# Attention's value weight multiplied by its output weight once on chip: the read comes out by tokens, the output product and its copy are left out, and all queues stand in a new order

## The reference, cut to what matters

```python
x = x + 0.5 * _L0_ffn_ref(_layernorm(x), ...)      # int8 product
x = x + _L0_attn_ref(_layernorm(x), ...)           # recurrence, then its feed-forward
x = x + 0.5 * _L0_ffn_ref(_layernorm(x), ...)
x = x + 0.5 * _L1_ffn_ref(_layernorm(x), ...)      # experts, pass 0
x = x + _L1_attn_ref(_layernorm(x), ...)
x = x + 0.5 * _L1_ffn_ref(_layernorm(x), ...)      # experts, pass 1
```

```python
q = hidden_state @ Wq + bq
k = jax.nn.sigmoid(hidden_state @ Wk + bk)
g = jax.nn.sigmoid(hidden_state @ Wg + bg)
v = hidden_state @ Wv + bv
def step(state, xs):
    qi, ki, vi, gi = xs
    state = state * gi[:, :, None] + ki[:, :, None] * vi[:, None, :]
    return (state, jnp.einsum('bk,bkv->bv', qi, state))
state, outs = jax.lax.scan(step, init, xs)
out = jnp.swapaxes(outs, 0, 1) @ Wo + bo
```

## Time and profile before

| | |
|---|---|
| median of 3 runs | 701.86 us (701.73 to 702.95) |
| profiled execution, first to last instruction | 703.3 us |
| instructions | 14597 |
| PE busy, PEld busy | 616.8 us (88%), 487.0 us (69%) |
| DVE, ACT, POOL busy | 487.2, 398.0, 387.9 us |
| mean granted clock of PE | 0.974 |
| chain that ended last, by engine | PE 59%, DVE 10%, ACT 9%, issue 7%, DMA 6% |

### The profile page before, as it was taken

One profiled execution on the slowest core, in us unless ns is written; L12 is line 12 of the kernel. 1 busy time (PEld: TensorE's weight loads), 2 busy tenths in 40 slices (PEclk: granted clock), 3 DMA queues, 4 the chain that ended last, 5 costly groups with the idle time before them and its releaser, 6 DMA issues.

```text
span 703.3 us, 14597 instructions
## 1 busy us (share of the span) xinstructions
PE 616.8 (88%) x4232; PEld 487.0 (69%) x4232; DVE 487.2 (69%) x1730; ACT 398.0 (57%) x1036; POOL 387.9 (55%) x416
## 2 busy tenths in 40 slices
PE   1478999999799989899986998899999999987971
PEld 1234565566566888788885886779878998776970
DVE  6986777878889867554625996878865874546334
ACT  3477887999686454554445556464665446343530
POOL 4425434435747787767653413651865764766642
PEclk9699999999999999999999999999999999999996
DMA  7998000000042366577668010214324545566886
GB/s 263 410 411 342 1 0 1 1 1 20 31 107 61 95 179 179 168 214 223 189 200 286 22 66 11 63 46 117 89 73 134 157 115 161 166 197 175 251 302 214
DMA packets 60126, 100.99 MB, mean 144 GB/s; under 512 B 10288, under 2 KB 28592, under 8 KB 59792
## 3 DMA queue, kind: packets, MB, share of 16 engines
q1 hardware_dynamic: 50832, 81.52, 37.7%
q0 software_dynamic: 8640, 17.84, 7.1%
q10 hardware_dynamic: 576, 0.69, 0.3%
HBM read 61.79 MB, written 38.23 MB: 142 GB/s over the span
## 4 chain that ended last, share of the span: by engine, by line
PE 59%; DVE 10%; ACT 9%; issue 7%; DMA 6%; POOL 5%; SPq 4%; POOLq 0%; ACTq 0%; DVEq 0%
PE bank L1071 14%; PE bank L1048 7%; PE bank L1282 4%; PE bank L934 3%; DMA tin<-rows_by_expert 3%; PE bank L959 3%; PE bank L308 3%; PE bank L945 3%; PE bank L510 3%; PE bank L663 3%; PE bank L313 3%; POOL rows_by_expert L830 2%; PE bank L677 2%; PE bank L1054 2%; PE bank L692 2%
## 5 line engine op out<-in xcount | busy, mean ns | idle before, releaser
L830 POOL DMA_INDIRECT rows_by_expert<-xx,sidx x128 | 126.3, 987 | 71.7 <-DVE xx L809 35.8
L1071 PE MATMUL bank<-tint,twt 128*128 128x128 f32 x1136 | 150.7, 278 | 10.9 <-DVE thidt L1109 5.7
L1071 PEld LDWEIGHTS bank<-tint,twt 128*128 128x128 f32 x1136 | 138.6, 192 | 26.3 <-issue 13.6
L1109 DVE TENSOR_TENSOR thidt<-tsil,bank 128x256 f32<-128x256 f32 x142 | 58.9, 419 | 98.6 <-ACT tsil L1087 86.6
L1120 POOL DMA_INDIRECT rows_done<-tout,tin x98 | 95.4, 974 | 52.4 <-ACT tout L1095 28.3
L1087 ACT ACTIVATE tsil<-bank 128x256 f32<-128x256 f32 x142 | 54.4, 384 | 82.1 <-PE bank L1071 80.4
L1048 PE MATMUL bank<-e_dn,thidt 128*128 x568 | 89.8, 283 | 7.3 <-issue 3.5
L1048 PEld LDWEIGHTS bank<-e_dn,thidt 128*128 128x128 f32 x568 | 76.4, 193 | 19.4 <-issue 18.8
L1095 ACT ACTIVATE tout<-bank,tin 128x128 f32<-128x128 f32 x142 | 51.5, 367 | 35.1 <-PE bank L1054 33.7
L1120 POOL DMA_INDIRECT rows_done<-tout,tdst x44 | 43.8, 996 | 30.1 <-issue 11.8
L1080 ACT ACTIVATE tint<-bank 128x128 f32<-128x128 f32 x142 | 38.2, 275 | 37.1 <-PE bank L1054 36.8
(11 more groups left out here) (271 smaller groups left out, 1363.9 us busy)
## 6 DMA issues: line engine op xcount, KB each, us to landing
twt<-moe_gu SPq DMA_DIRECT2D x142, 256.0 KB
rows_by_expert<-tout SPq DMA_DIRECT2D x25, 715.0 KB, 19.6
tin<-rows_by_expert SPq DMA_DIRECT2D x142, 65.0 KB
hid<-rows_done SPq DMA_DIRECT2D x12, 512.0 KB, 4.8
x<-x_in SPq DMA_DIRECT2D x8, 256.0 KB, 4.1
rows_by_expert<-xx,sidx POOLq DMA_INDIRECT x128
out<-x SPq DMA_DIRECT2D x8, 256.0 KB, 3.5
rows_done<-tout,tin POOLq DMA_INDIRECT x98, 3.0
```

The lines of the kernel that those rows point to most:

```text
L830: pool.indirect_dma_start(out=rows_by_expert, out_offset=bass.IndirectOffsetOnAxis(ap=sidx[h][:, k:k + 1], axis=0), in_=xx[h][:, r, t, :], ...
L1071: m = pe.matmul(bank[UP_BANKS[p][j]][:, c * P:(c + 1) * P], weights[:, c * P:(c + 1) * P], tint[g % TURNS][:, :], start=True, stop=True)
L1109: dve.tensor_tensor(thidt[g % TURNS][:, :, :].rearrange("p j c -> p (j c)"), tsil[g % TURNS][:, :], bank[UP_BANKS[p][j]][:, INNER:2 * INNE ...
```

## The change

`w_vo` holds the product of the value weight and the output weight (128 x 128) and, in each of its 128 rows, the value bias times the output weight. It is made once, on chip: two transposes (`k_vturn_tensor`), a copy, two products (`k_fold_tensor`) and a copy, between helpers of units 6 and 7 of the feed-forward block. `g_value_tensor` and `g_value_vector` use it in place of the value weight and bias. `g_read_tensor` exchanges its operands, so that the result comes out by tokens; `g_read_scalar` and `g_out_tensor` are gone, and `g_add_vector` adds the read's bank. `g_turn_tensor` now waits for that addition.

```diff
+        w_vo = sb("w_vo", [P, 2, P])
...
+            elif p == 0:
+                pe.wait_ge(s_voc, 2)
...
             if u >= 2:
-                pe.wait_ge(s_oc, n(u) - 2)
+                pe.wait_ge(s_x, n(u) - 2)
             transposes(pe, gb(u, 0), tt[u % 2], ident).then_inc(s_gtr, 1)
...
-                m = pe.matmul(gb(u, 0)[:, t * P:(t + 1) * P], gxt[u % 2][:, t * P:(t + 1) * P], a_sq[:, 2, :],
+                m = pe.matmul(gb(u, 0)[:, t * P:(t + 1) * P], gxt[u % 2][:, t * P:(t + 1) * P], w_vo[:, 0, :],
...
-                pe.matmul(gb(u, 0)[:, c0:c0 + P], v[:, c0:c0 + P], at[h][:, c0:c0 + P], start=True, stop=True)
-                pe.matmul(gb(u, 0)[:, c1:c1 + P], v[:, c0:c0 + P], across[h][:, b, :], start=True, stop=False)
-                m = pe.matmul(gb(u, 0)[:, c1:c1 + P], v[:, c1:c1 + P], at[h][:, c1:c1 + P], start=False, stop=True)
+                pe.matmul(gb(u, 0)[:, c0:c0 + P], at[h][:, c0:c0 + P], v[:, c0:c0 + P], start=True, stop=True)
+                pe.matmul(gb(u, 0)[:, c1:c1 + P], across[h][:, b, :], v[:, c0:c0 + P], start=True, stop=False)
+                m = pe.matmul(gb(u, 0)[:, c1:c1 + P], at[h][:, c1:c1 + P], v[:, c1:c1 + P], start=False, stop=True)
...
-        def g_read_scalar(act, u):
-            act.wait_ge(s_o, n(u))
-            if u >= 2:
-                act.wait_ge(s_op, n(u) - 2)
-            act.activation(bufE[u % 2][:, :], gb(u, 0)[:, :], ACT.Copy).then_inc(s_oc, 1)
-
-        def g_out_tensor(pe, u):
-            pe.wait_ge(s_oc, n(u))
-            tile_mm(pe, gb(u, 1), bufE[u % 2], a_sq[:, 4, :]).then_inc(s_op, 1)
-
         def g_add_vector(dve, u):
-            dve.wait_ge(s_op, n(u))
+            dve.wait_ge(s_o, n(u))
             dve.wait_ge(s_xbo, n(u))
-            dve.tensor_tensor(xu(u), xu(u), gb(u, 1)[:, :], ALU.add).then_inc(s_x, 1)
+            dve.tensor_tensor(xu(u), xu(u), gb(u, 0)[:, :], ALU.add).then_inc(s_x, 1)
...
+        def k_vturn_tensor(pe):
...
+            pe.transpose(bank[0][:, 0:P], a_sq[:, 2, :], ident)
+            pe.transpose(bank[0][:, P:2 * P], rows[:, R_BV:R_BV + P], ident).then_inc(s_vo, 1)
...
+        def k_fold_tensor(pe):
+            pe.wait_ge(s_voc, 1)
+            pe.matmul(bank[0][:, 0:P], across[0][:, 0, :], a_sq[:, 4, :], start=True, stop=True)
+            pe.matmul(bank[0][:, P:2 * P], across[0][:, 1, :], a_sq[:, 4, :], start=True, stop=True).then_inc(s_vo, 1)
```

The lists of all five engines are new from the first unit to the last; the rest of the diff is that. Two of their lines:

```diff
-            for j in range(0, 2):
+            for j in range(0, 5):
                 t_load_sync(sp_, 0, j)
```

More of the change, by code:

```diff
@@ L1504, in _ @@
+            t_weights_sync(sp_, 0, 18)
+            t_load_sync(sp_, 0, 23)
+            for j in range(19, 23):
+                t_weights_sync(sp_, 0, j)
+            t_load_sync(sp_, 0, 24)
+            for j in range(23, 25):
+                t_weights_sync(sp_, 0, j)
+            t_load_sync(sp_, 0, 25)
+            t_weights_sync(sp_, 0, 25)
+            for j in range(26, 28):
                 t_load_sync(sp_, 0, j)
-            for j in range(14, 17):
+            for j in range(26, 28):
@@ L1680, in _ @@
-            for j in range(41, 45):
+            for j in range(41, 43):
                 t_load_sync(sp_, 1, j)
@@ L2092, in _ @@
-            for j in range(58, 62):
+            for j in range(59, 62):
                 x_hid_vector(dve, 0, j)
@@ L2817, in _ @@
-            e_up_tensor(pe, 4, 0, 1)
-            for j in range(18, 20):
-                x_io_tensor(pe, 0, j)
+            q_mul_tensor(pe, 7, 1)
+            for j in range(9, 12):
+                x_up_tensor(pe, 0, j)
+            for j in range(12, 15):
+                x_io_tensor(pe, 0, j)
+            e_gate_tensor(pe, 4, 0, 0)
+            x_up_tensor(pe, 0, 12)
+            x_io_tensor(pe, 0, 15)
+            e_up_tensor(pe, 4, 0, 0)
+            x_up_tensor(pe, 0, 13)
+            r_logits_tensor(pe, 5, 0)
@@ L3511, in _ @@
             x_silu_scalar(act, 0, 12)
-            x_out_scalar(act, 0, 11)
-            for j in range(15, 17):
+            x_out_scalar(act, 0, 10)
+            for j in range(14, 16):
                 x_in_scalar(act, 0, j)
@@ L3626, in _ @@
+            for j in range(45, 47):
+                x_silu_scalar(act, 0, j)
+            for j in range(42, 44):
+                x_out_scalar(act, 0, j)
+            for j in range(48, 50):
+                x_in_scalar(act, 0, j)
+            x_silu_scalar(act, 0, 47)
+            for j in range(44, 46):
+                x_out_scalar(act, 0, j)
+            for j in range(50, 52):
+                x_in_scalar(act, 0, j)
+            x_out_scalar(act, 0, 46)
             e_silu_scalar(act, 7, 0, 1)
-            x_silu_scalar(act, 0, 46)
@@ new lines, in _ @@
+            x_out_scalar(act, 0, 48)
+            x_in_scalar(act, 0, 54)
+            for j in range(49, 52):
+                x_out_scalar(act, 0, j)
+            for j in range(52, 55):
+                x_silu_scalar(act, 0, j)
+            x_in_scalar(act, 0, 55)
+            x_out_scalar(act, 0, 52)
+            for j in range(56, 59):
+                x_in_scalar(act, 0, j)
+            x_out_scalar(act, 0, 53)
+            x_silu_scalar(act, 0, 55)
+            x_out_scalar(act, 0, 54)
+            x_silu_scalar(act, 0, 56)
@@ L3801, in _ @@
-            g_copy_scalar(act, 6)
+            g_cross_scalar(act, 5)
+            r_rows_scalar(act, 3, 1)
+            x_silu_scalar(act, 1, 5)
+            e_silu_scalar(act, 3, 1, 0)
+            g_copy_scalar(act, 6)
+            g_copy_scalar(act, 7)
+            for j in range(7, 9):
+                x_in_scalar(act, 1, j)
+            g_query_scalar(act, 6)
+            g_query_scalar(act, 7)
+            x_out_scalar(act, 1, 2)
             e_silu_scalar(act, 3, 1, 1)
-            x_silu_scalar(act, 1, 5)
@@ L3815, in _ @@
[L3815 to L3822 removed]
+            x_in_scalar(act, 1, 9)
+            for j in range(4, 6):
+                x_out_scalar(act, 1, j)
+            r_xt_scalar(act, 4, 1)
+            x_out_scalar(act, 1, 6)
+            for j in range(10, 12):
+                x_in_scalar(act, 1, j)
```

2648 lines of the change are left out of this document (1228 added, 1420 removed).

## The result

The changed kernel is slower: a median of 718.06 us (715.24 to 719.0, 4 runs) against 702.4 for the kernel before on the same chip (701.73 to 708.17, 4 runs). The ratio is 1.0191, 95% interval 1.0142 to 1.0239 (the quotient of the two medians is 1.022). Forecast were 693.5 us and a gain. The profiled execution took 719.0 us, its span 717.2.

A forecast was written before the change was run, and what follows sets the result against it. PE's instruction list was taken to bound the middle, 57 to 688 us. Terms -7.1 + 0.7 - 2.0 - 1.0 + 1.0 made -8.4 us, from 701.86 to 693.5 us, range 687.0 to 701.0.

The forecast's parts named there:

- Output products: Attention: eight output products of 0.89 us leave PE's list, -7.1 us, bounds 0 and -7.7.
- the first rival: Whole kernel: PE is not the bound and removed work turns into standing; 701.86 us within a microsecond, chance 0.07.
- The rule on weight loads: PE's headroom: weight-load share, 69% over the span, leaves a third of PE free; the removed products would be worth nothing.
- Fold: Two transposes and two products on PE, made once: +0.7 us, bounds +0.7 and +1.5.
- Exchange of operands: Attention's reads: same PE work, new wait replaces an old one; 0, bounds -0.5 and +0.7 per change of pair.
- Before the read of unit 2: Attention: normalizations leave ACT's chain where PE stood 0.69 + 1.65 us; -2.0 us, bounds 0 and -3.2.
- The start: Before the recurrence's first output product: minima and maxima move behind DVE's scan; -1.0 us, bounds -2.7 and +2.
- Table loads: ACT: 36 loads become 29, 9.0 us less, but PE covers them; 0, bound -1.5.
- SP's queue: Weight fetches, tile loads and last stage: waits stay, 0; bounds -1 and +2, -1.8, and -1 and +3.
- New waits: Throughout: the new order closes some of PE's 39.9 us of standing and opens others; +1.0 us, bounds -4 and +6.
- the first sign in the forecast: Profile after the change: PE busy about 610 us, from 616.8 less 7.1 plus 0.7.
- The slower rival: Recurrence, between two units' gate activations: ACT's batches leave PE without work; 705.5 us, chance 0.10.

The follow-up runs named there:

- the old order: Fold, exchanged read and missing output products, every queue ordered as in the kernel before; against that kernel 0.9998 and, again, 0.9968.
- the two kernels with calls moved: Fold in the old order, unit 2's addition earlier on DVE, unit 7's transposes later on PE: 1.0021 of the kernel before; with the new start also, 0.9977.
- The joins: Fold with new order only in part, against the kernel before: start and recurrence 0.9945, pass 0's experts 1.0057, up to attention 1.0055, from attention on 1.0054.
- the new start with the two moves: Fold with two calls moved, new order up to the feed-forward block's last down product, old order from there: 0.9977 of the kernel before.
- the cut in the new order: Changed kernel with POOL's 24 wide bias additions cut to 128 x 4, against the kernel before: 1.0077 and 1.0081 on slower chips, 0.9932 at 705 us.

## Why the prediction was wrong

Two steps failed: the worth of the removed products, put at 7.1 us and measured at 0 to 0.3% of the time in the old order, and the price of a new order, put at +1.0 us and measured at 13.9 us of standing and 7.1 of clock. Term by term:

*Output products, -7.1.* The work went: eight groups of 0.89 us. Its worth was the step that failed first. I took "PE never stood before any of its 64 instructions (0.0 us)" for proof that it was load. That tells what was ready before the products, not whether what stands behind them is ready when they go. The lower bound I gave, "0, if PE then waits where they stood", is what the old order showed: level within 0.3%, and in the two kernels with calls moved, on a chip at 705 us, standing up by 6.1 and 7.6 us. That is the first rival, to which I gave 0.07. The rule on weight loads that I set aside (Trainium skill, Perfetto Trace Analysis, Identifying the Most-Contended Engine) gave the nearer number for the old order; that a third of PE is free is not shown by it, since PE stands only 39.3 of 631 us there.

*Fold, +0.7.* Not measured by itself; in the two traces read for it, the changed kernel's and the old order's, PE does not stand before it.

*Exchange of operands, 0, with the new wait.* The read itself is unchanged: unit 2's starts at 467.94, and PE's next instruction at 469.27, 1.33 us. The wait was priced at 0 to 0.7 for each of three changes of pair. In the new order it is 0; in the old it was 3.09 and 1.90 us. What I called a wait "in the place of one for ACT's 597 ns copy" is one for an instruction in DVE's queue, behind whatever stands there, and for POOL's bias.

*Before the read of unit 2, -2.0.* Right at its place: 0.69 + 1.65 us became 0.21.

*The start, -1.0.* The first output product of the recurrence began at 55.45, 0.7 us later than in the earlier trace rows. Small. The joins and the new start with the two moves say that the new order of this part is good for 0 to 0.5%; in the traces PE ends the feed-forward block's last down product 1.1 us sooner (229.87 for 230.98).

*Table loads, 0.* ACT's busy time fell by 9 us (I had forecast 13 with the copies), and no gain of PE's can be put down to it.

*SP's queue, 0.* The standstill of 3.71 us is one of 2.31 at 384.20. In the last stage it was worse than its bounds: PE stands 4.15 us for a tile's rows at 688.72, where it was 1.62, and runs at half the clock for 6.1 us behind it: 2.5 + 3.0, 5.5 us; I had 0, at most +3. The shared expert's second product behind the last tile (703.02) cost nothing: the end comes 14.0 us behind that tile, before it was 15.2.

*New waits, +1.0, bounds -4 and +6.* The term that decided the sign. The standing rose by 13.9 us, and half the clock cost 7.1 us more than before, for which this term had nothing: a standstill was priced at its length, where the five places show 1.7 to 3.0 us on top (half of PE's busy time at half clock). I had read the clock behind one standstill in the earlier trace rows and used it for that place alone. With it went the first sign in the forecast: PE's busy time was to be about 610 us and is 623.5. Nor did I look at VectorE's longest instructions: the trace before already held 13.3 us of stretch, with one instruction of 2.04 us, so that any new order deals these collisions anew.

*The slower rival.* Right in its sign alone, and that is luck. Its time, 705.5, is 12.6 us short, and its place is wrong: at the end of the recurrence's feed-forward block PE was early, not late.

*The resolution.* I took 0.2% for what a measurement can tell apart; the interval reaches 0.5% to either side. The result lies far outside either.

The sum by measured terms, to the last tile: -6.4 of work, -1.9 of work now behind it, +13.9 of standing, +7.1 of clock, +2.4 of busy time without a cause shown: 15.1 us.

## What to carry to other kernels

Work that leaves the busiest engine's list is a gain only as far as what stands behind it is ready that much sooner; look at the next few items of the list and at when their last input arrives, not at the wait before the work that goes. A new order of all queues is no neutral carrier for a small edit: measure the edit in the old order first. And price a standstill of the matrix engine with the slower clock that often follows, as a possible cost and not a sure one.

## What the runs showed of the hardware

An elementwise VectorE instruction on SBUF tensors can stand still while GpSimd works: 3.33 and 3.00 us instead of 0.42, ending 0.3 us behind two additions of 1.25 us. All 23 stretched DVE instructions of the changed kernel overlap a POOL instruction; one of them (0.41 us for 0.17, at 631.86) meets nothing but an indirect DMA's 0.96 us. With POOL's bias additions cut, those that met them are gone, and ten are left beside POOL's other work (seven in each of the two earlier runs of that kernel). But a meeting is no sure stop: of the 70 DVE instructions of all kinds that began inside one of POOL's 128x512 elementwise instructions 17 were stretched, and of the 60 on 128x256 f32 SBUF tensors that began inside an indirect DMA three were. The Trainium skill (SBUF — State Buffer, SBUF: two separate sides) says that the two engines share a pair of ports as an exclusive lock (VectorE where it has two SBUF inputs or works in a mode that uses both ports) and that the loser fully blocks. The trace agrees with the full block. By the same section the one that starts first has the pair for the whole instruction. Here the two longest began while POOL was in an indirect DMA (until 244.32 and 412.14), and then let two additions pass that began after them; the one at 443.98 let a single addition pass and ended while POOL's next was running. What decides how many pass stays open.

PE's granted clock fell to half behind standstills of 1.99 to 4.15 us, for 3.4 to 6.1 us behind them, and twice, behind 2.77 and 2.07 us, not at all. In the kernel before it fell behind 3.71 and 1.65 us, and in its second trace, on another chip, it did not behind 2.46 and 2.45 us (326.49 and 377.02). So in these traces the length of a standstill alone does not tell.

And the kernel before took 702 to 705 us on some chips and 810 to 820 on others, with ratios between kernels that differ by more than their intervals (the cut in the new order: 1.008 and 0.993).
